# A fused attention and routed feed-forward kernel: where two late rows' slots place the score maxima of the next row

## The chip, the cores and the metric

The kernel runs on one core of one Trainium2 chip. The metric is the device time of one execution in microseconds (us); the median of three runs of the kernel before is 433.74 us.

## The reference

Eight rows (batch entries) of 256 tokens by 256 features pass through an attention layer and a feed-forward layer, each with a layer norm ahead of it and behind it:

```python
ct_q = lin(x, w_down_q); q = lin(ct_q, w_up_q) + rope(lin(ct_q, wq_r))      # 16 heads of 16
ct_kv = lin(x, w_down_kv); k = lin(ct_kv, w_up_k) + rope(lin(ct_kv, wk_r)); v = lin(ct_kv, w_up_v)
a = softmax(q @ k.T / 4) @ v ; x = x + layernorm(lin(a, wo))
logits = xn @ router_w.T                       # xn = layernorm(x); the best of 8 experts per token
shared = (silu(xn @ sg) * (xn @ su)) @ sd ; routed = expert(xn * sigmoid(top logit))
x = x + layernorm(shared + routed)
```

## The kernel before

Each of the five engines has its own instruction stream, written out in order; semaphores alone hold them together. There is no planner: the order of the work is a table per engine, and all engines walk the same tables.

**Slots and heads.** The attention part is a loop over eight slots, b = 0 to 7 (`run_attention`, L406), one for each row, and each slot has 16 heads, h = 0 to 15 (`run_slot`, L385). In head h every engine first does its `head` step: TensorE (PE) makes the scores of that head of row b in two bf16 products (L1576) and ScalarE (ACT) takes their exponentials (L873). The scores bank alternates between two, so the products of head h wait for the exponential of head h-2. Behind every fourth head PE multiplies four heads' probabilities with the values (`quad`, L1556, 16 products; here "PV").

**Maxima ahead.** The softmax subtracts a maximum that is found one slot ahead: in slot b the "units" (L367) make the scores of row b+1, 16 units a row, and in the kernel before one unit a head. A unit is two bf16 products on PE (`sm_scores`, L1517) into one of two banks and one reduction on VectorE (DVE, `sm_max`, L1057). Unit u waits for the reduction of unit u-2, which frees its bank (L1514). When eight units are reduced, GpSimd (POOL) splits that half of the maxima into three bf16 parts in four small instructions (`m_split`, L656: step M0 for the first half, M1 for the second), PE turns them (`m_turn`, L1522), ACT copies them out of the bank and issues the DMA that puts them under the queries (`mT_out`, L845). Scores of heads 0 to 7 need the first half in place, heads 8 to 15 the second.

**Other rows' steps.** Between the heads stand steps of other rows, by the tables `order` of each engine. In slot b: "A" steps make queries and keys of row b+2 (PE L1429 to L1461; ACT A_ev, A_khigh, A_qhigh, A_kmid, A_qmid; POOL A_kres, A_qres, A_klow, A_qlow; SyncE then stacks the parts in 24 DMAs, L536); "N" makes the values of row b+1; "D" finishes the attention of row b-1: D_avT0 and D_avT1 (PE turns, DVE divides, L1064 and L1068), D_aT (PE turns, ACT copies, L880), D_wo on PE (L1615, eight fp32 products, in the trace under the helper's line L1388), D_y on DVE (L1077, statistics, variance L1081), D_power on POOL (L641), D_yn on DVE (L1087), D_x1 on POOL (L675), D_stats on DVE (L991 to L1095), D_power2 on POOL; "E" takes row b-2: E_xn2 on DVE (L1104), E_xn2T on PE (in the trace under L1392), E_router. So E_xn2 of the row whose D steps are in slot b is taken in head 1 of the next slot, and PE turns it in head 3 there (in slot 7, which has its own table `last`, in head 2). An engine works its table strictly in order, within a head first the units and then the steps.

**Banks.** The turned maxima of both halves go to bank w2 (in the last row's second half to w0), which the D steps use as well; so M0 stands in head 12, behind D_wo, and PE waits there for `y_ready` (L1535).

**After the slots.** A written-out list of steps (`play`) covers the last rows' steps and the shared expert: X:n is the turn of routed token tile n on PE, x:n its copy on ACT, GR:8 gate and up products of the first routed tile, s:8 its silu, Y:n a down product.

Of the kernel before, what the change touches and what calls it, by code (L numbers as in the profile page):

```python
# [15 lines left out]

# [14 lines left out]
B, S, D = 8, 256, 256  # L31
NH, HD = 16, 16
# [84 lines left out]
def program(nc, x, const, w_down, w_q, w_kv, w_rope, w_out, w_router, bias_col, bias_v, bias_o,  # L117
# [6 lines left out]
    with ExitStack() as ctx:  # L124
# [166 lines left out]
        def m_bank(b, half):  # L291
            return w0 if (b, half) == (B - 1, 1) else w2

# [72 lines left out]

        def units(b, h):  # L367

            if b:
                return ((1, h),)
            if h < 9:
                return () if h else ((0, NH - 1),)
            u = 2 * (h - 9) + (h == NH - 1)
            return tuple((1, n) for n in range(u, u + 2 + (h >= NH - 2)))
# [6 lines left out]

        def run_slot(b, par, head, steps, order, last, behind):  # L385
            for h in range(NH):
                head(b, par, h)
                if b == B - 1:
                    play(steps, last.get(h, ""))
                    continue  # L390
                for ahead, u in units(b, h):
                    if exists(b + ahead):
                        steps["SM"](b + ahead, (par + ahead) % 2, u)
                for name in order.get(h, ()):
                    if not (b == 0 and name in MOVED):
                        step_of(steps, name, b, par)
                for n, names in FIRST_ROW.get(h, ()) if b == 0 else ():
                    for name in names.split():
                        if name in steps:
                            steps[name](n, n % 2)  # L400
                for name in MOVED:
                    if b == 0 and MOVED[name] == h and name in steps:
                        step_of(steps, name, b, par)
                behind(b, par, h)

        def run_attention(eng, head, steps, order, last, behind=lambda *_: None):  # L406

            for n, names in PROLOGUE:
                for name in names.split():
                    if name[0] == "S":
                        steps["SM"](0, 0, int(name[1:]))
                    elif name in steps:
                        steps[name](n, n % 2)
            for b in range(B):
                run_slot(b, b % 2, head, steps, order, last, behind)

# [213 lines left out]
        def _(pool):  # L633
# [38 lines left out]
            def add_x(b, par):  # L672
# [10 lines left out]
                "D_x1": add_x,  # L683
                "D_power2": lambda b, par: power("ff", b + 1, rstd2[:, ds(TB * b, TB)], var["ff"][:, :], TB),
                "SM": nothing}
            order = {0: ("M1",), 2: ("B_power",), 8: ("A_kres", "M0",),
                     9: ("A_qres",), 10: ("A_klow",), 11: ("A_qlow",), 12: ("D_power",), 13: ("D_x1",),
                     15: ("D_power2",)}

            def top_score(n, par):  # L690
# [20 lines left out]
            steps["L"] = routed_tile  # L711
            last = {0: "M1:7", 1: "E_score:0 D_power:6 D_x1:6 D_power2:6"}

            run_attention(pool, nothing, steps, order, last)
            play(steps, "D_power:7 D_x1:7 D_power2:7 E_score:1"
# [41 lines left out]
        def _(act):  # L757
# [124 lines left out]
            def xn2T_copy(b, par):  # L882
                act.wait_ge(sm["xn2T_ps"], b + 1)
                if counted(b):
# [13 lines left out]
                     5: ("A_ev0",), 6: ("A_ev1",), 7: ("A_khigh",), 8: ("A_qhigh",), 9: ("D_aT", "A_kmid",), 10: ("B_xnT", "A_qmid",),  # L898
                     12: ("C_o0",), 13: ("M0",), 14: ("B_ct",)}

            def xT_copy(seq, p):
# [18 lines left out]
            def unit_copy(seq, n, side):  # L920
# [5 lines left out]

            run_attention(act, head, steps, order, last)
            play(steps, "D_o1:7 E_xn2T:6 s:0 D_aT:7 s:1 y:0 s:2 y:1 E_xn2T:7 s:3 y:2 s:4 y:3"
                        " s:5 y:4 s:6 w:8 y:5 s:7 y:6 x:8 w:9 y:7 s:8 x:9")

# [27 lines left out]
        def _(dve):  # L958
# [149 lines left out]
            def d_router(b, par):  # L1108
# [10 lines left out]
                     6: ("D_div0",), 8: ("D_div1",), 9: ("N_v",), 11: ("D_y",),  # L1119
                     12: ("D_yn",), 14: ("D_stats",)}  # L1120


# [160 lines left out]
            steps["w"] = tile_first  # L1283
            run_attention(dve, nothing, steps, order, last)
            play(steps, "D_div0:7 c:4 c:5 E_router:6 D_div1:7 h:0 c:6 c:7 c:8 c:9 D_y:7 h:1 D_yn:7 D_stats:7 h:2 E_xn2:7"
# [97 lines left out]
        def _(pe):  # L1383
# [138 lines left out]
            def m_turn(b, par, half):  # L1522
# [8 lines left out]
                elif b < 2:  # L1531
                    if counted(2 * b):
                        pe.wait_ge(sm["mT_sb"], 2 * b)
                else:
                    pe.wait_ge(sm["y_ready"], b - 1)  # L1535
# [102 lines left out]
            def d_router(b, par):  # L1638
                pe.wait_ge(sm["xn2T_sb"], b + 1)
                for t in range(TB):  # L1640
# [11 lines left out]
                     6: ("D_avT0",), 8: ("D_avT1", "N_v",), 9: ("D_aT", "B_xnT",), 10: ("D_wo",),  # L1652
                     12: ("M0", "B_ct",), 13: ("B_ct1",)}

            def ranks(n, par):
# [151 lines left out]
            def first_routed(s, p):  # L1807
# [11 lines left out]

            run_attention(pe, head, steps, order, last, behind)  # L1820
            play(steps, "PV3:7 E_xn2T:6 D_avT0:7 E_router:6 D_avT1:7 G:1 D_aT:7 D_wo:7 U:1 Y:0 G:2 U:2 Y:1"
                        " E_xn2T:7 G:3 E_router:7 U:3 K:1 Y:2 G:4 U:4 Y:3 G:5 U:5 Y:4"
                        " G:6 U:6 I:0 Y:5 G:7 U:7 Y:6 X:8 Y:7 GR:8 X:9")

# [85 lines left out]
```

## Time and profile before

| what | before |
|---|---|
| time, median of 3 runs (lowest to highest) | 433.74 us (433.12 to 434.48) |
| time of the profiled execution | 429.76 us |
| span of the profiled execution | 427.9 us |
| TensorE busy | 397.9 us, 93% of the span |
| TensorE's granted clock, mean | 0.985 of full speed |
| VectorE, ScalarE, GpSimd busy | 273.4, 208.1, 129.6 us |

The span is from the first to the last instruction of one profiled execution; that execution's own time is 1.86 us more. Slot 5 runs in that trace from 154.2 to 178.7 us, slot 6 from there to 199.9, slot 7 up to about 219. Busy shares of TensorE are those of a pipelined engine; what it waits for is told by the idle time noted behind a group of instructions.

### The profile page before, as it was taken

How to read it: one execution, taken by the hardware profiler on the slowest of the kernel's cores; microseconds unless marked ns; L12 is line 12 of the kernel's file. 1: busy time of each engine (PE TensorE's matmuls, PEld its weight loads, DVE VectorE, ACT ScalarE, POOL GpSimd, SP SyncE). 2: the span in 40 equal slices, each digit the busy share in tenths (PEclk: the TensorE clock that was granted, in tenths of full speed). 3: DMA queues.
4: the chain of work that ended last, by engine and by line, in shares of the span. 5: the costliest groups of instructions: out<-in, count | busy, mean ns of one | idle time of the engine just before them, and what ended most of it. 6: DMA issues, size and time to landing. Idle time of an engine off the chain costs nothing.

```text
span 427.9 us, 9422 instructions
## 1 busy us (share of the span) xinstructions
PE 397.9 (93%) x3383; PEld 299.3 (70%) x3383; DVE 273.4 (64%) x629; ACT 208.1 (49%) x383; POOL 129.6 (30%) x184
## 2 busy tenths in 40 slices
PE   7998789999999999797989999999999999999990
PEld 6675456676776767374668999999994444589990
DVE  5674478787879786877475594222225898727775
ACT  1644647676675858555561112444446766311110
POOL 1423412516253434303211101212212220026872
PEclk9999899999999999899999999999999999999997
DMA  8899326364553736460127660011111111123422
GB/s 263 204 116 122 62 70 194 87 175 136 153 156 89 216 96 209 100 199 1 52 98 230 223 215 25 26 51 51 50 51 44 44 45 35 51 59 104 141 95 86
DMA packets 50756, 47.29 MB, mean 111 GB/s; under 512 B 5334, under 2 KB 45526, under 8 KB 50710
## 3 DMA queue, kind: packets, MB, share of 16 engines
q1 hardware_dynamic: 44779, 38.31, 34.2%
q0 software_dynamic: 1632, 4.46, 3.6%
q10 hardware_dynamic: 4299, 3.92, 2.7%
q8 instruction: 28, 0.46, 0.5%
q14 instruction: 18, 0.15, 0.1%
HBM read 25.19 MB, written 8.65 MB: 79 GB/s over the span
## 4 chain that ended last, share of the span: by engine, by line
PE 79%; DVE 8%; DMA 4%; issue 3%; ACT 3%; POOL 2%; ACTq 0%; DVEq 0%; POOLq 0%
PE bank L1388 40%; PE bank L1707 7%; PE bank L1392 6%; PE bank L1576 6%; PE bank L1556 5%; PE bank L1517 5%; PE bank L1732 3%; DMA stacks<-mT 2%; PE bank L1455 2%; DVE nmax L1057 2%; PE bank L1445 2%; PE bank L1503 1%; DVE wall L1087 1%; DVE stats_at L991 1%; POOL rstd_at L641 1%
## 5 line engine op out<-in xcount | busy, mean ns | idle before, releaser
L1057 DVE TENSOR_REDUCE nmax<-bank 128x2 f32<-128x512 f32 x112 | 74.4, 686 | 26.4 <-PE bank L1517 25.6
L1388 PEld LDWEIGHTS bank<-stacks,wall 128*128 128x128 f32 x512 | 59.8, 192 | 2.5 <-issue 1.9
L1388 PE MATMUL bank<-stacks,wall 128*128 128x128 f32 x512 | 61.2, 276 | 0.4 <-ACT stacks L909 0.4
L1263 DVE TENSOR_TENSOR stacks<-stacks,bank 128x512 f32<-128x512 f32 x34 | 23.3, 687 | 51.7 <-PE bank L1388 49.1
L873 ACT ACTIVATE pv<-bank 128x512 f32<-128x512 f32 x64 | 38.3, 603 | 36.7 <-PE bank L1576 35.8
L1576 PE MATMUL bank<-stacks 99*128 99x256 bf16 x256 | 49.5, 276 | 3.8 <-DMA stacks<-mT 3.3
L873 ACT ACTIVATE wall<-bank 128x512 f32<-128x512 f32 x64 | 38.5, 606 | 27.2 <-PE bank L1576 26.2
L909 ACT ACTIVATE stacks<-bank 128x512 f32<-128x512 f32 x34 | 20.3, 597 | 64.3 <-PE bank L1388 54.3
L1517 PE MATMUL bank<-stacks 96*128 96x256 bf16 x224 | 43.2, 278 | 6.4 <-DVE nmax L1057 6.2
L1388 PE MATMUL bank<-wall,stacks 128*128 128x256 f32 (+1 forms) x208 | 49.2, 380 | 0.0
L706 POOL DMA_INDIRECT stacks<-x_sc,row_i x18 | 19.9, 1105 | 89.5 <-PE bank L1392 70.5
L1388 PEld LDWEIGHTS bank<-wall,stacks 128*128 128x128 f32 x208 | 37.6, 190 | 4.1
L1576 PEld LDWEIGHTS bank<-stacks 99*128 99x128 bf16 x256 | 21.6, 100 | 26.3 <-issue 13.4
L1388 PEld LDWEIGHTS bank<-stacks,pv 128*128 128x128 f32 x320 | 37.2, 192 | 1.2 <-ACT stacks L903 0.7
L1388 PE MATMUL bank<-stacks,pv 128*128 128x128 f32 x320 | 37.4, 275 | 0.5 <-ACT stacks L903 0.5
L1707 PE MATMUL bank<-wall,stacks 128*32 x64 | 30.1, 595 | 0.5 <-ACT wdo_sb L922 0.5
L1517 PEld LDWEIGHTS bank<-stacks 96*128 96x128 bf16 x224 | 20.7, 99 | 13.7 <-DVE nmax L1057 10.8
L647 POOL TENSOR_TENSOR wall<-wall,low_sb 128x512 f32<-128x512 f32 x14 | 16.1, 1159 | 40.9 <-ACT low_sb L839 40.9
L721 POOL DMA_INDIRECT pv<-y_exp,back_i x16 | 16.2, 1010 | 33.7 <-DMA y_exp<-stacks 29.7
L1392 PE MATMUL bank<-cst,wall 128*128 128x128 f32 x160 | 24.2, 278 | 2.0 <-DVE wall L1104 0.8
L1392 PEld LDWEIGHTS bank<-cst,wall 128*128 128x128 f32 x160 | 18.0, 142 | 6.0 <-issue 2.4
L1271 DVE COPY pv<-wall 128x1024 f32 x24 | 16.7, 694 | 4.4 <-PE bank L1732 1.7
(207 smaller groups left out, 795.4 us busy)
## 6 DMA issues: line engine op xcount, KB each, us to landing
stacks<-low_sb SPq DMA_DIRECT2D x144, 64.0 KB, 2.5
wall<-gate_up SPq DMA_DIRECT2D x8, 1024.0 KB, 5.4
wall<-down SPq DMA_DIRECT2D x8, 512.0 KB, 6.9
y_exp<-stacks ACTq DMA_DIRECT2D x18, 128.0 KB, 1.7
x_tok<-wall SPq DMA_DIRECT2D x8, 256.0 KB, 2.5
stacks<-x_tok SPq DMA_DIRECT2D x16, 128.0 KB, 2.5
out<-stacks SPq DMA_DIRECT2D x8, 256.0 KB, 2.1
stacks<-low_sb SPq DMA_DIRECT2D x12, 128.0 KB, 5.9
```

What stands on the lines that cost most here:

```text
L706: pool.indirect_dma_start(out=xl[:, par, :], out_offset=None, in_=x_sc, in_offset=bass.IndirectOffsetOnAxis(ap=row_i[:, s - R0:s - R0 + 1] ...
L873: act.activation(probs[h // QUAD % 2][:, h % QUAD, :], st_bank[h % 2][:, :], ACT.Exp, scale=SCALE).then_inc(sm["exp_done"], 1)
L909: act.activation(sg, fg[:, :], ACT.Silu).then_inc(sm["sg_sb"], 1)
L1057: dve.tensor_reduce(nmax[:, half, qt, 2 * pair:2 * pair + 2], two(sm_bank[u % 2]), AX.X, ALU.max, negate=True).then_inc(sm["sm_max"], 1)
L1263: dve.tensor_tensor(to, sg, fu[:, :], ALU.mult).then_inc(sm["h_sb"], 1)
L1271: dve.tensor_copy(to, of).then_inc(sm[("gate_dve", "up_dve", "down_dve")[side]], 1)
L1388: last = pe.matmul(out_ap, lhsT, rhs, start=(n == 0), stop=(n == len(pairs) - 1))
L1392: return pe.transpose(out_ap, in_ap, ident)
L1517: last = pe.matmul(two(sm_bank[u % 2])[:, c, :], stacks[0:ROWS, par, 0, place(h), P * qt:P * qt + P], stacks[0:ROWS, par, 1, place(h), :], ...
L1556: last = pe.matmul(two(av_bank)[32 * c:32 * c + 32, g % 2, :], v_aug[:, par, k, QUAD * g + c, :], probs[g % 2][:, c, S * k:S * k + S], sta ...
L1576: last = pe.matmul(two(st_bank[h % 2])[:, k, :], stacks[0:MROWS, par, 1, place(h), P * k:P * k + P], stacks[0:MROWS, par, 0, place(h), :], ...
L1707: last = pe.matmul((fg, fu)[r][U * n:U * n + U, :], xT[:, p, P * k + U * n:P * k + U * n + U], w, start=(k == 0), stop=(k == KT - 1))
```

## The change

In slots 5 and 6 (b = B-3 and B-2) each engine uses a second table, `late`. There the units of the next row no longer come one a head but two a head in some heads, so that they end in head 10 (slot 5) and 11 (slot 6). M0 of the next row is split in head 7, turned in head 9 into bank w0 and copied in head 10. POOL splits the second half (M1) in head 12 of the same slot, ahead of D_x1, and no longer at the start of the next. The D steps and E_router move one head forward. In the last list X:9 and x:9 move ahead of GR:8 and s:8.

```diff
         def m_bank(b, half):
-            return w0 if (b, half) == (B - 1, 1) else w2
+            return w0 if (b, half) in ((B - 2, 0), (B - 1, 0), (B - 1, 1)) else w2
...
+        EVEN = at_heads(*[1] * NH)
+        UNITS_AT = {B - 3: at_heads(1, 1, 2, 1, 1, 1, 1, 2, 2, 2, 2),
+                    B - 2: at_heads(0, 1, 1, 1, 1, 2, 1, 1, 2, 2, 2, 2)}
...
             if b:
-                return ((1, h),)
+                heads = UNITS_AT.get(b, EVEN)
+                return tuple((1, u) for u in heads[h]) if h < len(heads) else ()
...
-        def run_slot(b, par, head, steps, order, last, behind):
+        def run_slot(b, par, head, steps, order, last, behind, late):
+            if b in UNITS_AT:
+                order = late
...
                 "D_power2": lambda b, par: power("ff", b + 1, rstd2[:, ds(TB * b, TB)], var["ff"][:, :], TB),
+                "M1_sixth": lambda b, par: m_split(b, par, 1) if b == B - 3 else None,
+                "N_M1": lambda b, par: m_split(b, par, 1),
...
+            late = {0: ("M1_sixth",), 7: ("M0",), 8: ("A_kres",), 9: ("A_qres",), 10: ("A_klow",), 11: ("A_qlow",),
+                    12: ("D_power", "N_M1"), 13: ("D_x1",), 15: ("D_power2",)}
...
-            last = {0: "M1:7", 1: "E_score:0 D_power:6 D_x1:6 D_power2:6"}
+            last = {1: "E_score:0 D_power:6 D_x1:6 D_power2:6"}
...
+            late = {2: ("M1",), 3: ("E_xn2T",), 4: ("D_o1",), 5: ("A_ev0",), 6: ("A_ev1",), 7: ("A_khigh",),
+                    8: ("D_aT", "A_qhigh",), 9: ("A_kmid",), 10: ("M0", "A_qmid",), 12: ("C_o0",)}
...
-                        " s:5 y:4 s:6 w:8 y:5 s:7 y:6 x:8 w:9 y:7 s:8 x:9")
+                        " s:5 y:4 s:6 w:8 y:5 s:7 y:6 x:8 w:9 y:7 x:9 s:8")
...
+            late = {1: ("A_T", "E_xn2"), 4: ("E_router",), 5: ("D_div0",), 7: ("D_div1",), 8: ("N_v",), 10: ("D_y",),
+                    11: ("D_yn",), 13: ("D_stats",)}
...
+                elif b >= B - 2:
+                    pe.wait_ge(sm["k_sb"], 2 * B)
+                    pe.wait_ge(sm["mT_sb"], 2 * b)
...
+            late = {0: ("A_R",), 1: ("A_Q",), 2: ("M1", "A_QK",), 3: ("E_xn2T",), 4: ("E_router",), 5: ("D_avT0",),
+                    7: ("D_avT1", "N_v",), 8: ("D_aT",), 9: ("M0", "D_wo",)}
...
-                        " G:6 U:6 I:0 Y:5 G:7 U:7 Y:6 X:8 Y:7 GR:8 X:9")
+                        " G:6 U:6 I:0 Y:5 G:7 U:7 Y:6 X:8 Y:7 X:9 GR:8")
```

The last five `late` tables and lists belong, in this order, to ACT (table and list), DVE (table) and PE (table and list); the one before them to POOL.

## Rows read from the trace of the kernel before

**Rows 1.** The page: busy time, share of the span, instructions of each engine.

```profile
PE 397.9 (93%) x3383; PEld 299.3 (70%) x3383; DVE 273.4 (64%) x629; ACT 208.1 (49%) x383; POOL 129.6 (30%) x184
```

**Rows 2.** PE in time: start us, us, line, what, idle before and its cause.

```profile
163.73 0.38 PE L1576 MATMUL bank<-stacks 99*128 99x256 bf16 x2
163.95 0.38 PE L1517 MATMUL bank<-stacks 96*128 96x256 bf16 x2
...
168.75 1.99 PE L1388 MATMUL bank<-wdo_sb,wall 128*128 128x256 f32 x8 [0.25 <-ACT wall L880]
...
170.80 0.38 PE L1517 MATMUL bank<-stacks 96*128 96x256 bf16 x2
...
174.55 0.39 PE L1517 MATMUL bank<-stacks 96*128 96x256 bf16 x2 [0.84 <-DVE nmax L1057]
...
176.25 0.60 PE L1517 MATMUL bank<-stacks 96*128 96x256 bf16 x2 [1.09 <-DVE nmax L1057]
176.78 1.94 PE L1556 MATMUL bank<-pv 128*32 128x256 f32 x16
...
181.83 0.66 PE L1392 MATMUL bank<-cst,wall 128*128 128x128 f32 x4 [0.23 <-DVE wall L1104]
182.41 1.07 PE L1556 MATMUL bank<-wall,pv 128*32 128x256 f32 x16
...
191.11 1.99 PE L1388 MATMUL bank<-wdo_sb,wall 128*128 128x256 f32 x8 [0.25 <-ACT wall L880]
...
196.90 0.39 PE L1517 MATMUL bank<-stacks 96*128 96x256 bf16 x2 [0.84 <-DVE nmax L1057]
...
198.60 0.39 PE L1517 MATMUL bank<-stacks 96*128 96x256 bf16 x2 [1.08 <-DVE nmax L1057]
...
202.42 0.66 PE L1392 MATMUL bank<-cst,wall 128*128 128x128 f32 x4 [0.57 <-DVE wall L1104]
```

**Rows 3.** DVE in time, slots 5 and 6.

```profile
171.22 0.69 DVE L1057 TENSOR_REDUCE nmax<-bank 128x2 f32<-128x512 f32 x1 [1.68 <-PE bank L1517]
171.83 0.68 DVE L1077 TENSOR_TENSOR wall<-bank,bo_sb 128x512 f32<-128x512 f32 x1
...
173.81 0.68 DVE L1057 TENSOR_REDUCE nmax<-bank 128x2 f32<-128x512 f32 x1
...
175.51 1.28 DVE L1057 TENSOR_REDUCE nmax<-bank 128x2 f32<-128x512 f32 x2
...
194.19 0.68 DVE L1077 TENSOR_TENSOR wall<-bank,bo_sb 128x512 f32<-128x512 f32 x1
...
196.08 0.17 DVE L1081 TENSOR_SCALAR var_at<-mv_at 128x2 f32<-128x2 f32 x1
```

**Rows 4.** Windows: us, busy us of PE, PEld, DVE, ACT, POOL, granted clock, DMA.

```profile
172.00:176.00 4.00, 2.32 (x20) 1.23 (x16) 3.57 (x10) 2.59 (x6) 1.03 (x2) 1.00 0.41 103
176.00:180.00 4.00, 3.75 (x27) 1.68 (x28) 2.85 (x9) 0.98 (x3) 2.31 (x6) 0.57 0.36 89
...
194.00:198.00 4.00, 2.68 (x28) 1.29 (x20) 3.57 (x11) 2.24 (x5) 0.70 (x1) 1.00 0.00 0
198.00:202.00 4.00, 3.26 (x40) 1.37 (x40) 3.41 (x10) 1.85 (x5) 2.44 (x4) 1.00 0.01 3
```

**Rows 5.** ACT in time, end of slot 5.

```profile
174.39 0.73 ACTq L859 DMA_DIRECT2D stacks<-mT  x1
175.22 1.08 ACT L873 ACTIVATE wall<-bank 128x512 f32<-128x512 f32 x2 [0.86 <-PE bank L1576]
```

**Rows 6.** POOL in time: first and last instruction of one split of maxima.

```profile
179.06 0.20 POOL L663 CAST mparts<-nmax 128x16 bf16<-128x16 f32 x1
...
179.90 0.22 POOL L669 TENSOR_TENSOR mparts<-nres,mparts 128x16 bf16<-128x16 f32 x1
```

**Rows 7.** PE in time at the first routed tiles.

```profile
273.43 0.82 PE L1388 MATMUL bank<-stacks,pv 128*128 128x128 f32 x5 [0.47 <-ACT stacks L903]
```

More of the change, by code:

```diff
@@ L15 @@
 from contextlib import ExitStack
+from itertools import accumulate
 import numpy as np
@@ L365, in step_of, with at_heads @@
                 steps[name](b + ahead, (par + ahead) % 2)
+        def at_heads(*counts):
+            ends = list(accumulate(counts))
+            assert ends[-1] == NH
+            return [range(e - c, e) for c, e in zip(counts, ends)]
+        EVEN = at_heads(*[1] * NH)
+        UNITS_AT = {B - 3: at_heads(1, 1, 2, 1, 1, 1, 1, 2, 2, 2, 2),
+                    B - 2: at_heads(0, 1, 1, 1, 1, 2, 1, 1, 2, 2, 2, 2)}
         def units(b, h):
             if b:
-                return ((1, h),)
+                heads = UNITS_AT.get(b, EVEN)
+                return tuple((1, u) for u in heads[h]) if h < len(heads) else ()
             if h < 9:
@@ L404, in run_slot, with run_attention @@
                 behind(b, par, h)
-        def run_attention(eng, head, steps, order, last, behind=lambda *_: None):
+        def run_attention(eng, head, steps, order, last, behind=lambda *_: None, late=None):
             for n, names in PROLOGUE:
@@ L417, in run_attention @@
             for b in range(B):
-                run_slot(b, b % 2, head, steps, order, last, behind)
+                run_slot(b, b % 2, head, steps, order, last, behind, late or order)
         def nothing(*_):
@@ L711, in _ @@
             steps["L"] = routed_tile
-            last = {0: "M1:7", 1: "E_score:0 D_power:6 D_x1:6 D_power2:6"}
-            run_attention(pool, nothing, steps, order, last)
+            last = {1: "E_score:0 D_power:6 D_x1:6 D_power2:6"}
+            run_attention(pool, nothing, steps, order, last, late=late)
             play(steps, "D_power:7 D_x1:7 D_power2:7 E_score:1"
@@ L925, in _ @@
             last = {2: "D_o1:6", 3: "E_xn2T:5", 5: "M1:7", 6: "D_aT:6", 10: "C_o0:7"}
-            run_attention(act, head, steps, order, last)
+            run_attention(act, head, steps, order, last, late=late)
             play(steps, "D_o1:7 E_xn2T:6 s:0 D_aT:7 s:1 y:0 s:2 y:1 E_xn2T:7 s:3 y:2 s:4 y:3"
-                        " s:5 y:4 s:6 w:8 y:5 s:7 y:6 x:8 w:9 y:7 s:8 x:9")
+                        " s:5 y:4 s:6 w:8 y:5 s:7 y:6 x:8 w:9 y:7 x:9 s:8")
             def body(seq, n, p, kinds):
@@ L1283, in _ @@
             steps["w"] = tile_first
-            run_attention(dve, nothing, steps, order, last)
+            run_attention(dve, nothing, steps, order, last, late=late)
             play(steps, "D_div0:7 c:4 c:5 E_router:6 D_div1:7 h:0 c:6 c:7 c:8 c:9 D_y:7 h:1 D_yn:7 D_stats:7 h:2 E_xn2:7"
@@ L1818, in _ @@
                     7: "D_wo:6", 8: "K:0", 9: "PV1:7 Ga:0", 10: "Gb:0", 11: "Ua:0", 12: "Ub:0", 13: "PV2:7"}
-            run_attention(pe, head, steps, order, last, behind)
+            run_attention(pe, head, steps, order, last, behind, late=late)
             play(steps, "PV3:7 E_xn2T:6 D_avT0:7 E_router:6 D_avT1:7 G:1 D_aT:7 D_wo:7 U:1 Y:0 G:2 U:2 Y:1"
                         " E_xn2T:7 G:3 E_router:7 U:3 K:1 Y:2 G:4 U:4 Y:3 G:5 U:5 Y:4"
-                        " G:6 U:6 I:0 Y:5 G:7 U:7 Y:6 X:8 Y:7 GR:8 X:9")
+                        " G:6 U:6 I:0 Y:5 G:7 U:7 Y:6 X:8 Y:7 X:9 GR:8")
             def body(seq, n, p, kinds):
```

## The prediction

> **What bounds the kernel now.** I read the page first: TensorE is busy 93% of the span [rows 1], so the time is its work plus the places where it is held. Nothing in the change takes work from it: the same units, turns and products are issued. Its effect is therefore the sum of the holds that go and the holds that come. For these I read PE in time over slots 5 and 6, looking only at groups with idle time before them [rows 2]. In each slot's end two units wait for a reduction: 0.84 and 1.09 us in slot 5, 0.84 and 1.08 us in slot 6. The next hold is in the following slot, where the turn E_xn2T waits for DVE's normalised row: 0.23 us before 181.83 and 0.57 us before 202.42. DVE in time [rows 3] says why the units wait. The reduction at 173.81 could have run at 172.8, but D_y and its statistics (from 171.83) stand ahead of it; the next pair (175.51) stands behind D_yn. So two chains share DVE at a slot's end: unit to reduction to unit, which holds PE, and D_wo, D_y, D_power, D_yn, D_x1, D_stats, D_power2, E_xn2, E_xn2T, which holds PE one slot on. The reader should see that the second one is the one that ends last: its whole length from D_y to the turn is 202.42 - 194.19 = 8.23 us in slot 6, of which D_y to the variance at 196.08 is 1.9 us. Between variance and turn only one slot edge lies, and PE arrives before the turn is ready in both slots.
>
> **Part 1: units two a head.** This removes the four holds in the slot ends, 0.84 + 1.09 + 0.84 + 1.08 = 3.85 us. That is the cover that goes from in front of E_xn2T, and what is late next is E_xn2T itself. To see how late, I walk slot 5 forward with these intervals: scores or a unit on PE take 0.22 us start to start (163.73 to 163.95 in [rows 2]); a unit's reduction can start 0.42 us after the unit (170.80 to 171.22 in [rows 2, 3]); reductions follow each other in 1.28 - 0.68 = 0.61 us and the unit that waits for one starts 0.06 us behind its end (173.81 + 0.68 = 174.49, unit 174.55); a PV group is 1.00 us, D_wo 1.83 to the next product, and D_y can start 2.03 us after D_wo begins.
>
> Two units a head are no longer spaced by PE's other work, so the second must wait for the reduction of unit u-2. In slot 5, head 7, unit 9 waits for the reduction of unit 7, which stands on DVE behind D_div0: about 0.75 us of hold on PE. PE then does unit 9, D_avT1, N_v, PV, head 8, units 10 and 11, D_aT, head 9, units 12 and 13, M0, and only then D_wo. Compared with before, D_wo has one head's scores less, but three units (0.66) and M0's turn (0.21 to 0.3) more ahead of it; with the hold it begins at 170.3 where it began at 168.75 [rows 2], 1.5 us later. D_y may start at 172.3. But it stands on DVE behind the reductions of units 14 and 15, whose products come behind D_wo and head 10: 172.35 + 0.42, two intervals, and D_y begins at 173.95 where it began at 171.83 [rows 3]. From there the chain is free of reductions: 8.23 us by slot 6 of before, and it ends at 182.2, against 181.83. So slot 5 gives up 0.4 us at the point where PE is held, although PE gets through heads 11 to 15 sooner and would be at that turn at 180.6.
>
> Slot 6 by the same walk: everything starts 0.4 later at its E_xn2T. Holds on paired units: D_avT1 waits for D_div0, which stands behind two reductions, 0.4; unit 7 0.15; unit 11 0.4. With M0's turn (0.3) D_wo begins at 192.6, before 191.11 [rows 2]. D_y could start at 194.6, but units 12 and 13 come from PE only behind D_wo (194.6 and 194.85), their reductions stand ahead of D_y and the first waits 0.42: D_y begins at 196.25, before 194.19. The reductions of 14 and 15 stand between the variance (198.15) and D_yn, and delay it by 0.3; POOL's split, below, adds 0.2. The turn of row 5 in slot 7 is ready at 196.25 + 8.23 + 0.5 = 205.0, against 202.42. That is **+2.6 us**, and it holds the 0.4 of slot 5. PE would be there at 202.8 and waits 2.2 us. Slot 7 is written as before and each of its later steps hangs on this turn or stands behind it on PE, so I let the 2.6 us pass whole to the end. The bounds: 0 if slot 7 takes it all up, 3.9 us if slot 5's 0.4 is doubled by slot 6's and each of the four removed holds comes back as a reduction wait.
>
> **Part 2: M0 in head 9, in bank w0.** No instruction is added; the turn moves from head 12 to 9, ahead of D_wo, and its 0.3 us stands in the sum above. Its DMA issue on ACT takes 0.73 us and moves ahead of A_qmid and the exponential of head 11 [rows 5]; with D_aT ahead of A_qhigh, row 7's parts for the queries reach POOL about 2 us later. POOL's A_qlow then ends at 176.0, just as D_power wants the engine, and the stack of DMAs for row 7 ends near 179.3, where unit 0 is wanted at 178.7: a wait of 0.6, hidden in front of the late E_xn2T. The scores of heads 0 wait for a DMA that now has three heads more: that costs nothing, and gave nothing before.
>
> **Part 3: M1 split a slot sooner.** Four POOL instructions from 179.06 to 179.90 + 0.22, 1.06 us [rows 6], now stand between D_power and D_x1. D_yn leaves POOL about 1.0 us of idle time there, so the cost is 0 to 0.1 in slot 5. In slot 6 the split waits for the reduction of unit 15 (199.5): D_x1 is 0.2 late, counted above. At the slot's start nothing on PE waited for the split, so its gain is 0. If D_yn came with no delay of its own, the split would cost up to 1.1.
>
> **Part 4: D steps and router a head sooner.** They issue the same instructions; what matters is in part 1: a head sooner in name is later in time, because the heads are fuller.
>
> **Part 5: X:9 ahead of GR:8.** Before, PE waited 0.47 us for the copy x:9 [rows 7]. Now the turn stands ahead of sixteen gate products and more, and the copy is hidden by them; the token tile had been in memory for some us. Gain 0.47, bounds 0 and 0.5.
>
> **The clock.** At the slot ends PE is sparse: 2.32 us busy in 172 to 176, then the granted clock in 176 to 180 is 0.57, nearly the lower level of 1.2 GHz, and a PV group takes 1.94 instead of 1.07 us [rows 4, 2]. After 2.68 busy us in 194 to 198 it stayed at 1.00, the level of 2.4 GHz [rows 4]. So one of two such stretches cost clock: 0.43 of 4 us, 1.7 us. In my walk the stretches ahead of both turns are emptier than either (about 1.9 of 3.7 us, then 1.3 of 3.6), and come where nothing else hides slow products. The bounds are 0 (one dip, as now) and 3.4 less the 1.7 of before plus 0.9 of cover lost, 2.6. I take half of one dip, **+0.85**: one more dip falls on the path and half of it lies in front of waits.
> The Trainium skill, in "TensorE: Matmul & The Clock Gate" (Part 1: The HAM clock gate), says that idling is what lowers the clock and that sustained activity must come first for it to rise. The two windows agree with the first only half, since one of two sparse stretches kept its clock. By the rule alone both turns would be followed by slow products, which is the third rival below.
>
> **Sum.** +2.6 - 0.45 + 0.85 = +3.0 us. Made against the profiled execution (429.76 us, 427.9 of it span) it gives 432.8; that execution is 4.0 us under the median of the runs, of which the profile shows no cause, and I carry the difference over: 433.74 + 3.0 = 436.7.
>
> **Rivals.**
> *The chain is not late.* If DVE takes the paired reductions without holding PE, D_wo keeps its place, and D_y's turn comes before the reductions that I put ahead of it, then PE's arrival decides: slot 6's turn comes at 180.6 instead of 181.83 and slot 7's at 201.2 instead of 202.42, 1.2 us sooner, and with X:9 -1.7: 432.0. It decides from the point where E_xn2 is done before PE arrives: my walk misses that by 1.6 us in slot 6 and by 2.2 in slot 7. For it: the holds of 3.85 us are real, and they do go. Against it: D_y has waited for its reduction even at one unit a head [rows 3].
> *Slot 7 or the reductions take up most of it.* Half of 2.6 us arrives, X:9 gives its part and no dip is added: +0.85, 434.6, no difference to be told. For it: 0.57 of PE's wait in slot 7 was there before; my intervals add up over forty steps.
> *Both turns are followed by low clock.* +2.6 - 0.45 + 2.6 = +4.75: 438.5. For it: the emptier stretches. Against it: slots 6 to 7 in the trace.
> *The change does nothing in the slots* (only X:9 counts): 433.3; it would need the 0.4 and 2.6 us both to be errors.
>
> **Chances.** About 0.3% (1.3 us) is what a measurement of this kernel can tell from none. My forecast (435.2 to 437.8) 0.43; both dips 0.18; slot 7 takes it up 0.14; nothing in the slots 0.07; not late 0.18. Slower then 0.61, the same 0.21, faster 0.18. The range leaves a tenth at each end: from 432.2, nearly the case where the chain is not late, to 439.2, both dips with a margin of 0.7. The likeliest sign's own range is 435.2 to 439.2.
>
> **What the next profile would show.** Right: no hold on units in the slot ends; holds of a few tenths on the second unit of heads 7 to 10; D_wo at about 170.3 and 192.6; D_y behind two reductions; PE idle over 1 us before E_xn2T near 182.2 and over 2 us near 205.0, and a granted clock under 0.8 behind one of them; no wait for the copy of X:9. Wrong: E_xn2T starting right behind the unit ahead of it; D_wo earlier than 169.5; D_y starting as soon as D_wo is done; slot 7 beginning and ending closer together than the 2.6 us allow.

## The result, and the profile after

The changed kernel takes 436.28 us (median of 14 runs, 433.26 to 441.68); the kernel before took 431.84 us in the 14 runs beside it (430.98 to 434.48). The ratio is 1.0096, 95% interval [1.0071, 1.0121]: slower, by 3.1 to 5.2 us. Executions more than 1.5% above the fastest of their kernel (two of these 14) are left out of the ratios and of the means further down. The profiled executions have spans of 434.9 us (mean granted clock 0.979) and 427.9 us (0.985).

First the page after, to be read beside [rows 1]:

```profile
PE 401.8 (92%) x3383; PEld 299.9 (69%) x3383; DVE 274.7 (63%) x629; ACT 208.1 (48%) x383; POOL 129.8 (30%) x184
```

The same 3383 products are issued; busy time grew 3.9 us without one product more (the mean clock is lower in this execution), and the span grew 7.0. The rest is waiting. Where, PE in time says (slots 5 and 6 of the changed kernel; columns as in [rows 2]):

```profile
155.61 0.39 PE L1598 MATMUL bank<-stacks 99*128 99x256 bf16 x2
...
166.54 0.39 PE L1536 MATMUL bank<-stacks 96*128 96x256 bf16 x2 [0.60 <-DVE nmax L1074]
...
171.70 1.99 PE L1407 MATMUL bank<-wdo_sb,wall 128*128 128x256 f32 x8
...
176.78 0.88 PE L1598 MATMUL bank<-stacks 99*128 99x256 bf16 x4 [0.88 <-ACT pv L888]
178.24 0.39 PE L1598 MATMUL bank<-stacks 99*128 99x256 bf16 x2 [0.58 <-ACT wall L888]
...
181.83 0.39 PE L1536 MATMUL bank<-stacks 96*128 96x256 bf16 x2 [1.65 <-DMA stacks<-low_sb]
...
183.91 0.96 PE L1411 MATMUL bank<-cst,wall 128*128 128x128 f32 x4 [0.49 <-DVE wall L1121]
184.80 1.93 PE L1578 MATMUL bank<-wall,pv 128*32 128x256 f32 x16
...
195.92 1.99 PE L1407 MATMUL bank<-wdo_sb,wall 128*128 128x256 f32 x8
...
199.14 0.39 PE L1536 MATMUL bank<-stacks 96*128 96x256 bf16 x2 [0.35 <-DVE nmax L1074]
...
202.15 0.39 PE L1598 MATMUL bank<-stacks 99*128 99x256 bf16 x2 [0.47 <-ACT wall L888]
203.12 0.39 PE L1598 MATMUL bank<-stacks 99*128 99x256 bf16 x2 [0.58 <-ACT wall L888]
...
208.64 0.65 PE L1411 MATMUL bank<-cst,wall 128*128 128x128 f32 x4 [2.26 <-DVE wall L1121]
...
277.80 4.96 PE L1407 MATMUL bank<-stacks,pv 128*128 128x128 f32 x43
```

The holds of 0.84 to 1.09 us in front of units [rows 2] are gone from both slot ends. In their place PE now waits further on: for the exponentials of the scores (0.88, 0.58, 0.47, 0.58), for the transfer of the low parts (1.65), and above all in front of the turn E_xn2T of row 5 (2.26, before 0.57). The 0.47 us of [rows 7] do not appear behind the early X:9.

Slot 5 begins at 155.61, before at 154.21. These 1.40 us arose where nothing was changed: a low clock (0.53) from 33.8 to 41 put this execution 2.76 us behind, and one in the kernel before, at 44 to 52 (0.80 and 0.77 in its two halves), gave half of that back. I subtract the 1.40 to compare. D_wo then stands at 170.30 and 194.52 (before 168.75 and 191.11). DVE in time, same kernel:

```profile
174.17 1.29 DVE L1074 TENSOR_REDUCE nmax<-bank 128x2 f32<-128x512 f32 x2 [1.27 <-PE bank L1536]
175.38 0.68 DVE L1094 TENSOR_TENSOR wall<-bank,bo_sb 128x512 f32<-128x512 f32 x1
...
198.39 1.29 DVE L1074 TENSOR_REDUCE nmax<-bank 128x2 f32<-128x512 f32 x2 [1.27 <-PE bank L1536]
199.60 0.68 DVE L1094 TENSOR_TENSOR wall<-bank,bo_sb 128x512 f32<-128x512 f32 x1
...
201.57 1.28 DVE L1074 TENSOR_REDUCE nmax<-bank 128x2 f32<-128x512 f32 x2
202.77 0.87 DVE L1104 SCALAR_TENSOR_TENSOR wall<-wall,mv_at,rstd_at 128x256 f32<-128x256 f32 x2
```

D_y is at 173.98 and 198.20 (before 171.83 and 194.19 [rows 3]), each time straight behind a pair of reductions. POOL in time shows what else stands in that chain: the split of the second maxima ends just as D_yn is done, and D_x1 follows it:

```profile
202.92 0.38 POOL L674 CAST mparts<-nmax 128x16 bf16<-128x16 f32 x1 [0.48 <-DVE nmax L1074]
...
204.06 0.22 POOL L680 TENSOR_TENSOR mparts<-nres,mparts 128x16 bf16<-128x16 f32 x1
204.24 1.27 POOL L686 TENSOR_TENSOR x_sb<-x_sb,wall 128x512 f32<-128x512 f32 x1
```

D_yn ends at 202.77 + 0.87 = 203.64, so D_x1 is 0.6 us late. Last the windows of the changed kernel (columns as in [rows 4]): from slot 5's start to E_xn2T of row 4, from there to E_xn2T of row 5, and four stretches of 4 us.

```profile
155.61:183.91 28.30, 23.80 (x208) 15.47 (x205) 19.91 (x47) 17.59 (x36) 10.59 (x20) 1.00 0.47 132
183.91:208.64 24.73, 20.43 (x174) 11.77 (x174) 15.83 (x36) 11.96 (x22) 4.60 (x11) 0.93 0.30 95
176.00:180.00 4.00, 2.54 (x26) 1.07 (x26) 2.16 (x8) 3.27 (x8) 3.35 (x7) 1.00 0.39 99
180.00:184.00 4.00, 1.86 (x15) 0.95 (x14) 2.89 (x9) 1.93 (x4) 1.47 (x2) 1.00 0.33 81
184.00:188.00 4.00, 4.00 (x30) 2.21 (x30) 1.33 (x3) 1.89 (x4) 0.00 (x0) 0.57 0.40 100
204.00:208.00 4.00, 2.39 (x34) 0.87 (x26) 1.46 (x6) 2.32 (x5) 2.16 (x3) 1.00 0.00 0
208.00:212.00 4.00, 2.98 (x28) 2.20 (x32) 1.77 (x6) 1.89 (x4) 0.00 (x0) 1.00 0.12 46
```

The same two stretches of the kernel before, and of the kernel that only has the early X:9 (its code in these slots is that of before):

```profile
154.21:181.83 27.62, 25.11 (x211) 16.31 (x207) 20.39 (x48) 17.47 (x36) 10.25 (x20) 0.94 0.51 143
181.83:202.42 20.59, 17.86 (x172) 11.42 (x172) 15.36 (x35) 11.24 (x22) 4.33 (x10) 1.00 0.32 104
```

```profile
156.85:183.65 26.80, 23.85 (x211) 15.95 (x207) 20.36 (x48) 17.46 (x36) 10.22 (x20) 1.00 0.51 142
183.65:205.03 21.38, 19.21 (x173) 11.81 (x173) 15.30 (x35) 10.71 (x20) 4.54 (x11) 0.92 0.35 107
```

From slot 5's start to E_xn2T of row 5: 53.03 us changed, 48.21 before, 48.18 in the third, each with one stretch of low clock. That is +4.8 us over before; PE's idle time in them is 48.21 - 42.97 = 5.2 us before and 53.03 - 44.23 = 8.8 changed. Behind the first routed tiles the distance has shrunk by 0.7 (from 6.23 us there to 5.49). In the last output tiles this one execution loses another 1.5, in waits that no step of the change touches; I did not find their cause.

### The profile page after: what moved, and what is told of

Its sections match the earlier page's. It is cut to its first block, busy times and chain, and to the rows that moved or that the text cites. A ratio compares the mean times of both kernels' runs of the same rounds, so it can differ in the third digit from the quotient of the medians.

```text
span 434.9 us, 9422 instructions
## 1 busy us (share of the span) xinstructions
PE 401.8 (92%) x3383; PEld 299.9 (69%) x3383; DVE 274.7 (63%) x629; ACT 208.1 (48%) x383; POOL 129.8 (30%) x184
## 4 chain that ended last, share of the span: by engine, by line
PE 70%; DVE 11%; POOL 5%; issue 5%; DMA 4%; ACT 3%; SPq 1%; ACTq 1%; DVEq 0%; POOLq 0%
PE bank L1407 36%; PE bank L1731 7%; PE bank L1411 5%; PE bank L1578 4%; PE bank L1598 4%; PE bank L1536 4%; PE bank L1756 3%; DVE nmax L1074 3%; PE bank L1474 2%; PE bank L1522 1%; PE bank L1464 1%; SPq L547 1%; DMA stacks<-mT 1%; DVE stacks L1377 1%; POOL pv L736 1%
## 5 line engine op out<-in xcount | busy, mean ns | idle before, releaser
L1536 PE MATMUL bank<-stacks 96*128 96x256 bf16 x224 | 41.7, 274 | 5.9 <-DVE nmax L1074 4.0
L1536 PEld LDWEIGHTS bank<-stacks 96*128 96x128 bf16 x224 | 19.8, 98 | 14.6 <-DVE nmax L1074 9.6
```

The source lines that it names most:

```text
L1536: last = pe.matmul(two(sm_bank[u % 2])[:, c, :], stacks[0:ROWS, par, 0, place(h), P * qt:P * qt + P], stacks[0:ROWS, par, 1, place(h), :], ...
```

## The experiments

The last two columns of this table come from the list of each kernel's executions, which gives the span S and the mean granted clock c (as a share of full speed) of each. S(1-c) is the **lost clock**, Sc the span without it; means over the runs, with their standard error. The experiments ran in three sets of four, each with its own runs of the kernel before beside it, whose Sc and lost clock were 421.1 ± 0.2 and 9.9 ± 0.5 (x9_only to dy_first), 421.7 ± 0.2 and 9.2 ± 0.3 (pack_only to mild), 421.5 ± 0.1 and 9.5 ± 0.3 (the last four). So a difference between kernels of different sets is uncertain by another 0.5 us or so. The split is rough: across the runs of one kernel 1 us of lost clock goes with 0.5 to 1.0 us of span. The traces show one reason, that a low clock in front of a wait costs less: the 1.7 us lost in slot 5 of before (0.43 of 4 us) made the way to the turn of row 4 only 0.8 us longer (27.62 for the 26.80 of the third kernel).

```
kernel        median us   ratio to before [95%]       Sc            lost clock
changed       436.28      1.0096 [1.0071, 1.0121]     424.8 ± 0.2    9.2 ± 0.5
x9_only       432.31      0.9986 [0.9956, 1.0015]     420.5 ± 0.3   10.3 ± 0.5
even_units    434.16      1.0026 [0.9992, 1.0061]     422.0 ± 0.4   10.0 ± 0.6
m1_late       438.35      1.0142 [1.0085, 1.0199]     423.7 ± 0.5   13.0 ± 1.2
dy_first      438.24      1.0146 [1.0084, 1.0207]     424.4 ± 0.5   11.5 ± 1.6
pack_only     433.76      1.0020 [0.9985, 1.0054]     422.0 ± 0.3    9.8 ± 0.6
steps_only    433.52      1.0000 [0.9969, 1.0032]     421.7 ± 0.3    9.5 ± 0.4
slot6_even    434.52      1.0043 [1.0013, 1.0072]     422.9 ± 0.4    9.5 ± 0.6
mild          431.75      0.9959 [0.9924, 0.9995]     421.0 ± 0.3    8.2 ± 0.7
turn_later    435.17      1.0047 [1.0015, 1.0078]     423.5 ± 0.3   10.2 ± 0.6
act_order     435.96      1.0082 [1.0047, 1.0116]     424.3 ± 0.4    9.5 ± 0.6
filled        430.55      0.9950 [0.9922, 0.9979]     421.4 ± 0.2    7.5 ± 0.4
combined      432.37      0.9985 [0.9955, 1.0016]     420.7 ± 0.2    9.4 ± 0.4
```

**x9_only.** The kernel before with X:9 ahead of GR:8, and the copy ahead of s:8 on ACT.

```diff
-" G:6 U:6 I:0 Y:5 G:7 U:7 Y:6 X:8 Y:7 GR:8 X:9"
+" G:6 U:6 I:0 Y:5 G:7 U:7 Y:6 X:8 Y:7 X:9 GR:8"
```

> The kernel before with X:9 ahead of GR:8 and x:9 ahead of s:8, nothing else. If the slots alone make the change slower, this one is 0.5 to 0.75 us faster than before (the wait of 0.47 us on PE goes, and the first routed tiles begin 0.7 us sooner behind the inverse). If the swap brings a new hold (the copy standing ahead of the silu), it is equal or slower.

0.9986 [0.9956, 1.0015]. The size agrees with the 0.47 us of [rows 7], the interval also with nothing. Sc is 0.7 ± 0.4 us lower. So the loss is in the slots. Against this kernel it is 4.0 us by the medians and 4.7 by the ratios.

**even_units.** The changed kernel with one unit a head in both slots; the second split back at its old place.

```diff
-UNITS_AT = {B - 3: at_heads(1, 1, 2, 1, ...), B - 2: at_heads(0, 1, 1, ...)}
+UNITS_AT = {B - 3: EVEN, B - 2: EVEN}
-late = {0: ("M1_sixth",), 7: ("M0",), ... 12: ("D_power", "N_M1"), ...}
+late = {0: ("M1",), 7: ("M0",), ... 12: ("D_power",), ...}
```

> The changed kernel with one unit a head as before and M1 split at the next slot's start as before; bank w0, M0 in head 9, the D steps a head sooner and X:9 stay. Theory (packed units hold PE and stand ahead of D_y): it falls to 0.5 to 1.5 us under before, D_y of slot 5 begins about 0.4 us sooner than in the kernel before, the units' holds of about 1 us come back in the slot ends. Rival (the moved steps, the DMA issue on ACT ahead of A_qmid, or bank w0 cost the time): it stays 2 to 4 us above before.

434.16 us; 1.0026, 2.1 us of median under the changed kernel and 1.9 over x9_only. Its trace has the holds of units back (0.97 and 0.91, 0.79 and 1.08 us). So the kernel that has those waits again is the faster one, and the packed spacing costs. The time lies between the two expectations, under the rival's and over the theory's: what stands beside the packing seems to cost something too, but against x9_only the intervals overlap.

**m1_late.** The changed kernel, units still packed, the second split back in the next slot's head 0.

> The changed kernel with M1 split at the next slot's start as before, all else changed. Theory (D_y behind the reductions is most of it, the split adds its wait ahead of D_x1): 0.3 to 0.6 us under the changed kernel, E_xn2T of row 5 still over 1.5 us late. Rival (the split is what delays the chain): 2 us or more under the changed kernel.

438.35 us, 2.1 over the changed kernel by the medians, where 0.3 to 0.6 under it was expected; the intervals of the ratios overlap. PE in time:

```profile
180.64 0.39 PE L1536 MATMUL bank<-stacks 96*128 96x256 bf16 x2 [1.73 <-DMA stacks<-low_sb]
182.69 0.39 PE L1559 MATMUL bank<-idb,mparts 128*24 128x128 bf16 x2 [1.21 <-POOL mparts L680]
...
209.83 0.66 PE L1411 MATMUL bank<-cst,wall 128*128 128x128 f32 x4 [1.75 <-DVE wall L1121]
```

The turn of the second maxima now waits 1.21 us for the split, while E_xn2T of row 5 waits 0.5 us less than in the changed kernel (1.75 for 2.26). The two columns part here: without lost clock this kernel is 1.1 ± 0.5 us shorter than the changed one, with 3.9 ± 1.3 us more of lost clock. So the early split saves a wait of 1.21 us, and a later one is longer with it (the low clock of this trace, from 180 to 194, may have a part in that). Whether it is worth anything is not shown: the higher median goes with the lost clock of six runs, and no run says whether the new wait brought it.

**dy_first.** m1_late with D_y and D_yn a head earlier on DVE, ahead of the reductions that they stood behind.

```diff
-8: ("N_v",), 10: ("D_y",), 11: ("D_yn",)
+8: ("N_v",), 9: ("D_y",), 10: ("D_yn",)
```

> The kernel of m1_late with D_y on DVE in head 9 and D_yn in head 10, so that the reductions of units 14 and 15 (slot 5) and 12 to 15 (slot 6) stand behind D_y; units stay two a head. Theory (the place of D_y behind the reductions costs about 1.6 us a slot): D_y of slot 5 begins 2.03 us after D_wo, and the time is 1.5 to 3 us under m1_late. Rival (the holds on PE from paired units, or the late stack of DMAs, cost the time): within 0.7 us of m1_late.

PE in time, slot 6 and the turn of row 5:

```profile
199.97 0.39 PE L1536 MATMUL bank<-stacks 96*128 96x256 bf16 x2 [1.88 <-DVE nmax L1074]
...
207.05 0.60 PE L1411 MATMUL bank<-cst,wall 128*128 128x128 f32 x4
```

The wait at E_xn2T is gone, and a unit waits 1.88 us instead; from slot 5's start to this turn it is 52.59 us, changed 53.03. At 438.24 us it is no faster than m1_late, where the theory wanted 1.5 to 3 us. The two chains on DVE trade places: with the reductions first the turn waits (1.75 in m1_late), with D_y first a unit does (1.88).

**pack_only** and **steps_only.** x9_only with the packed units and nothing else; and x9_only with D_avT, N_v, D_aT, D_wo, D_y and the router a head sooner and units as before.

> The kernel of x9_only (the one before with X:9 moved) with the units of slots 5 and 6 two a head as in the change, all step tables, banks and splits as before. Theory (packed units hold PE in pairs and put reductions ahead of D_y): 1.5 to 3 us over x9_only, of the 3.8 that the whole change costs beyond X:9. Rival (the packing is harmless by itself and the other moves cost the time): within 0.7 us of x9_only.

> The kernel of even_units with M0 back in heads 8, 12 and 13 and in bank w2, so that beside X:9 only the D steps, N_v and the router stand a head sooner. even_units was 1.5 us over x9_only. Theory (M0 ahead of D_wo and its DMA issue ahead of A_qmid on ACT make that): 0 to 0.7 us over x9_only. Rival (the steps a head sooner make it, by the wait of N_v for ACT's copy and of D_avT1 for D_div0): still 1 to 2 us over x9_only.

433.76 and 433.52 us: 1.4 and 1.2 over x9_only by medians (1.5 and 0.6 by ratios, intervals overlapping). The waits of pack_only:

```profile
177.48 0.61 PE L1577 MATMUL bank<-stacks 99*128 99x256 bf16 x4 [1.44 <-DMA stacks<-mT]
...
180.00 0.39 PE L1538 MATMUL bank<-idb,mparts 128*24 128x128 bf16 x2 [0.83 <-POOL mparts L670]
...
201.74 0.61 PE L1577 MATMUL bank<-stacks 99*128 99x256 bf16 x4 [1.03 <-DMA stacks<-mT]
...
205.44 0.66 PE L1393 MATMUL bank<-cst,wall 128*128 128x128 f32 x4 [1.76 <-DVE wall L1105]
```

Without the early M0 the scores of the next slot wait for the transfer of the maxima (1.44, 1.03): the changed kernel has no such wait. Neither part alone costs what the whole does, and pack_only stands at the lower edge of what was expected; even_units less steps_only, the early M0 and its bank, is 0.6 by medians. The three add up to 3.2 of the 4.0 us, but each of them is about as large as the uncertainty of a median, so this list is a rough one.

**slot6_even.** The changed kernel, slot 6 alone with one unit a head; row 7's second split is back at the start of slot 7.

> The changed kernel with one unit a head in slot 6 (its M1 split at the start of slot 7); slot 5 as changed. By the prediction's walk slot 6 makes 2.2 of the 2.6 us: then 1.5 to 2.5 us under the changed kernel. Rival: the cost is split evenly between the slots, and about 1 us comes off.

434.52 us, 1.8 under the changed kernel (intervals [1.0013, 1.0072] and [1.0071, 1.0121] barely touch; Sc is 1.9 ± 0.5 lower). Its E_xn2T of row 5 waits 0.24 us and not 2.26. So the spacing in slot 6, with the early split of row 7 that goes with it, makes nearly half of the loss.

**turn_later.** The changed kernel with row 5's turn E_xn2T behind D_avT1 of row 6 in the last slot; D_avT0, which now comes first, gets a wait of its own for D_y of the row before.

```diff
-last = {1: "PV3:6", 2: "E_xn2T:5", 3: "D_avT0:6", 4: "M1:7 D_avT1:6", ...}
+last = {1: "PV3:6", 3: "D_avT0:6", 4: "M1:7 D_avT1:6 E_xn2T:5", ...}
```

> The changed kernel with one step moved on TensorE: the turn of row 5's normed tile (E_xn2T, in slot 7) stands behind the second D_avT of row 6 at head 4, and not at head 2; its copy on ScalarE goes from head 3 to head 5. In the changed kernel TensorE waits 2.26 us for VectorE at this turn (208.64). Theory: this wait is the price of the late D chain of row 5, and work that is ready could stand in it; then the wait falls under 0.3 us and the kernel comes out 1.5 to 2.2 us under the changed one, at about 434.3. Rival: the wait hides later ones in the last slot (unit holds, the routed part's start), or the clock decides; then within 0.5 us of the changed kernel.

```profile
211.20 0.66 PE L1411 MATMUL bank<-cst,wall 128*128 128x128 f32 x4 [0.96 <-ACT wall L881]
...
212.91 1.09 PE L1411 MATMUL bank<-cst,wall 128*128 128x128 f32 x8 [0.63 <-DVE wall L1085]
```

435.17 us, 1.1 under the changed kernel, less than expected. The wait for VectorE's E_xn2 is gone, but the turn of the attention row that now comes first waits 0.96 us for ACT's copy, and the pair behind it 0.63. Further on the router's products wait 0.61 us for ACT (216.64), where in the changed kernel D_wo waited 0.36. Up to the first gate products the changed kernel waited 2.26 + 0.38 + 0.36 = 3.00 us, this one 2.20, and the way there from the PV group ahead of the first of these waits is 0.81 us shorter (12.79 from 208.63, 13.60 from 204.99), and Sc fell by 1.3 ± 0.4 (the intervals of the ratios still overlap by a hair). So the late chain of row 5 does cost time at the end, and this move fills only a part of the wait that it gives PE.

**act_order.** The changed kernel, high and middle parts of q ahead of the copies of D_aT and M0 on ACT.

```diff
-8: ("D_aT", "A_qhigh",), 9: ("A_kmid",), 10: ("M0", "A_qmid",)
+8: ("A_qhigh", "D_aT",), 9: ("A_kmid",), 10: ("A_qmid", "M0",)
```

> The changed kernel with two pairs exchanged on ScalarE in slots 5 and 6: the high parts of q (A_qhigh) ahead of the copy of D_aT in head 8, and the middle parts (A_qmid) ahead of the copy of M0 in head 10. It lets the low parts and their transfers start earlier by a copy or two. In the changed kernel unit 0 of row 7 waits 1.65 us for the transfer of the stacked low parts (181.83), and E_xn2T of row 4 behind it still 0.49 us for VectorE. Theory: the transfer's wait stands in front of a D chain that is as late, so it costs nothing; then within 0.5 us of the changed kernel, and the wait moves to E_xn2T. Rival: the transfer's wait is a cost of its own; then 1 to 1.5 us under the changed kernel.

```profile
182.78 0.66 PE L1411 MATMUL bank<-cst,wall 128*128 128x128 f32 x4 [0.61 <-DVE wall L1121]
```

```profile
154.53:182.78 28.25, 25.21 (x209) 15.97 (x205) 19.77 (x47) 17.60 (x36) 10.62 (x20) 0.94 0.45 133
182.78:205.93 23.15, 18.85 (x174) 11.20 (x175) 15.84 (x36) 11.94 (x22) 4.59 (x11) 1.00 0.32 101
```

The wait of 1.65 us for the low parts is gone, E_xn2T of row 4 comes 28.25 us behind slot 5's start (154.53), changed 28.30, and the median is 0.3 us lower. The longest single wait that the change brought to slot 5 was free: it stood in front of a later one. In this trace the low clock also falls ahead of the turn of row 4, and slot 6 has none: its 23.15 us to the turn of row 5 are the changed kernel's slot 6 at full clock.

**mild.** x9_only with two units in head 10 only, and none in head 15, in both slots.

> The kernel of x9_only with one unit moved: in slots 5 and 6 head 10 has two units, ahead of D_wo, and head 15 none; all else as before. DVE is idle 1.7 us behind D_wo there, so the eleventh reduction costs nothing, and the wait of the last unit for D_yn's row goes. Theory (what decides is which reductions stand ahead of D_y, and where DVE is idle): 0.5 to 2 us under x9_only. Rival (any unit ahead of D_wo delays the chain as much as it frees): equal or slower than x9_only.

```profile
175.02 0.39 PE L1518 MATMUL bank<-stacks 96*128 96x256 bf16 x2 [0.83 <-DVE nmax L1058]
...
177.54 0.39 PE L1577 MATMUL bank<-stacks 99*128 99x256 bf16 x2 [0.90 <-DMA stacks<-mT]
178.63 0.47 PE L1518 MATMUL bank<-stacks 96*128 96x256 bf16 x2 [0.70 <-DMA stacks<-low_sb]
```

431.75 us, 0.9959 [0.9924, 0.9995]: one hold of 0.83 instead of two in each slot, D_y not delayed, and transfers that now show (in slot 6 the turn of row 5 waits 1.56 us). Faster than the kernel before; not told apart from x9_only.

**combined.** mild with the first maxima turned in head 10, and turn_later's move.

> Mild spacing of the units (one a head up to head 9, two in head 10, none in head 15), X:9, the first maxima turned in head 10 behind D_wo into the bank w0 with its copy in head 11, and row 5's E_xn2T in slot 7 moved from head 2 to head 4 as in turn_later; all D steps stay at their old heads. Theory: what holds the mild kernel still is the wait of 1.56 us at E_xn2T of row 5 and the waits of 0.90 and 0.70 us for transfers that follow the maxima; with both eased it comes out 0.5 to 1.5 us under mild, at 430.3 to 431.3. Rival: the last slot's waits or the transfers take it up; then within 0.4 us of mild.

432.37 us, 0.6 over mild by the medians, where 0.5 to 1.5 under it was expected. The rival was nearer: unit 0 of the next row waits 1.73 us for the low parts, and no gain over mild is left.

**filled.** x9_only, with products that nobody reads in the idle time in front of units 14 and 15.

```diff
+if b >= B - 2 and u >= NH - 2:
+    pe.wait_ge(sm["v_ready"], b + 1)
+    for _ in range(10 if u == NH - 2 else 14):
+        pe.matmul(w1[:, 0:P], ones_bf[:, :], ones_bf[:, :], start=True, stop=True)
 pe.wait_ge(sm["sm_max"], ...)
```

> The kernel before with the early unit of slot 7 (X:9), and besides with 10 products of 128 x 128 ahead of unit 14 and 14 ahead of unit 15 in slots 5 and 6, into a bank that nothing reads: they fill most of the idle time in which TensorE waits for a score unit's maxima at a slot's end. Theory (the sparse stretch at the slot's end brings the low clock about 176 to 180 on some executions): the low clock there goes, the mean of the lost clock falls by 0.5 to 1.5 us, and the kernel comes out as much under x9_only, at 431 to 432. Rival: the lost clock is set by something else in the program; then no change against x9_only, or up to 1 us slower where the products delay the units.

PE in time at the end of slot 5, then two windows:

```profile
174.16 0.72 PE L1517 MATMUL bank<-ones_bf 128*128 128x128 bf16 x10
175.16 0.39 PE L1521 MATMUL bank<-stacks 96*128 96x256 bf16 x2 [0.28 <-DVE nmax L1057]
175.38 0.38 PE L1580 MATMUL bank<-stacks 99*128 99x256 bf16 x2
175.61 0.94 PE L1517 MATMUL bank<-ones_bf 128*128 128x128 bf16 x14
176.85 0.39 PE L1521 MATMUL bank<-stacks 96*128 96x256 bf16 x2 [0.30 <-DVE nmax L1057]
```

```profile
172.00:176.00 4.00, 3.72 (x50) 2.58 (x43) 3.57 (x10) 2.19 (x6) 0.90 (x2) 1.00 0.41 103
176.00:180.00 4.00, 3.20 (x38) 1.64 (x35) 3.64 (x10) 2.02 (x4) 2.18 (x4) 1.00 0.33 82
```

430.55 us, 0.9950 [0.9922, 0.9979]: the lowest median of all, faster than both kernels, 1.8 us under x9_only (their intervals overlap a little, as do those of filled and mild). It brings no unit forward: unit 14 stands 20.33 us behind the start of slot 5 (154.83), before 20.34. Against x9_only, what fell is the lost clock, from 10.3 ± 0.5 to 7.5 ± 0.4 us, a difference of 2.8 ± 0.6, while Sc rose by 1.0 ± 0.4. Those two ran in different sets; against the kernel before beside it the lost clock fell by 2.0 ± 0.5 and Sc stayed (421.4 and 421.5). The traces agree on the place: of the 14 kernels' profiled executions, only that of filled has its full clock all through slots 5 and 6; each of the other 13 has a stretch of low clock between 176 and 212 us. So the holds at the slot ends did cost something beside the waiting itself: they are sparse stretches, and slow products follow, as far as one trace of each kernel and the means of the lost clock can show it.

## Why the prediction was right, point by point

The forecast was 436.7 us, slower; measured 436.28. The mechanism was right: the chain to E_xn2T came late, by the reductions ahead of D_y, and PE waited there. That the figure came within 0.4 us is luck. Two terms were off in size and in part set each other off, and the base was high: I added +3.0 to a median of 433.74, which more runs put at 431.8 to 433.0, while the added time is 3.1 to 5.2.

**Part 1, the late D chain: right, under-sized.** Slot 5 came out as walked: D_wo 170.30 (walked 170.3), D_y 173.98 (173.95), E_xn2T 182.51 (182.2), the hold on the second unit 0.60 (0.75). In slot 6, D_wo came at 194.52 where I had 192.6: the low clock behind 184 lies in it (192.6, 0.3 for slot 5 and some 1.7 for 0.43 of 4 us make 194.6). PE's wait at the turn of row 5 is 2.26 (2.2). The wait at the turn of row 4 was forecast at over 1 us and is 0.49, because 1.65 us went to the transfer ahead of it. turn_later and slot6_even show that the wait of row 5 reaches the end, dy_first that putting D_y first on DVE does not win it back. The term of +2.6 was too small. The failed step is the comparison: I took "E_xn2T at 181.83" as what slot 5 of before takes, but that slot held a dip of the clock (176 to 180 at 0.57 [rows 4]). The same code without a dip takes 26.80 us to that turn (x9_only), not 27.62. Against 28.30 the loss of slot 5 alone is +1.5, not +0.4. The rows of before already held the hint: from D_y to the turn slot 5 took 181.83 - 171.83 = 10.00 us, slot 6 only the 8.23 that I carried over. For slot 6 at full clock there are two traces: 23.15 us in act_order, and in filled, whose steps of the slots are those of before, 20.56 (181.61 to 202.17). That is +2.6, where I had 2.2. Together the slots cost 1.5 + 2.6 = 4.1 us in the traces and 4.3 ± 0.4 by the means of Sc (changed less x9_only), for the 2.6 of the forecast.

**Part 2, the early M0: right for itself, blind to its gain.** The wait for the low parts came, 1.65 us for the 0.6 forecast, and is hidden as said (act_order). But "gave nothing before" is true only of the kernel before: with packed units and M0 at its old place PE waits 1.44 and 1.03 us for the maxima's transfer (pack_only).

**Part 3, the early split: its gain of 0 stays open.** With packed units 1.21 us of wait return without it (m1_late), and 0.5 us of a later one go; by the medians that kernel is 2.1 us slower, without lost clock it is 1.1 shorter. Its cost was under-sized: D_x1 is late by 0.6 in slot 6, 0.2 forecast.

**Part 4.** Costed at nothing beside part 1; steps_only puts it at 0.6 us (ratios) to 1.2 (medians) over x9_only with the old units, which is not told apart from none.

**Part 5, X:9: right.** The wait of 0.47 is gone, the distance between the traces shrinks by 0.7 there; the time of x9_only agrees, but is not told apart from no gain.

**The clock: +0.85 was wrong.** One stretch of low clock lies behind the turn of row 4 (0.57 in 184 to 188), none behind that of row 5, after 2.39 busy us of 4. That is one dip, as before, and the mean lost clock is 9.2 ± 0.5 (10.1 ± 0.8 over all 14 runs) against 9.5 ± 0.3: no change that can be told. I had priced the change in sparse stretches from two windows of one execution.
The Trainium skill, in "TensorE: Matmul & The Clock Gate" (Part 1: The HAM clock gate), says that idling is what lowers the clock; filled agrees with it (less idling, 2.0 to 2.8 us less lost clock). Which stretch is followed by the low clock can't be told from its busy time here: after 2.39 busy us of 4 (204 to 208, changed kernel) the clock stayed at 1.00, after 2.32 (172 to 176, before) it fell to 0.57.

**The rivals.** "Not late" and "nothing in the slots" fall with the 2.26 us and the 4.7 us over x9_only. "Slot 7 takes it up" falls with the distance of the traces: 6.22 us at the turn of row 5 and 6.23 just ahead of the routed tiles. "Both turns followed by low clock" didn't come in the profiled execution.

## What to carry to other kernels

Before a hold is removed, ask what the engine runs into next, and what the work that is brought forward takes from an engine that two chains share: here 3.85 us of holds went, PE's idle time over two slots still rose from 5.2 to 8.8 us, and neither order tried on DVE gave both chains their turn. When a walk is compared with a trace, first look whether the stretch it is compared with had its full clock; a dip in it hides as much of a loss as the dip cost. And a wait that can't be removed may still be worth filling with products that nobody reads, if the engine's clock falls behind it.

## What I had not expected

The largest gain found, 0.5%, is in executing more: with 48 products that nobody reads the lost clock is 2.0 ± 0.5 us (against before) to 2.8 ± 0.6 us (against x9_only) lower and the time about 2 us. Low clock is not a fixed property of the code: with the same instructions in the slots the dip was at 176 to 180 in the execution of before, and in slot 6 in that of x9_only (0.92 over 183.65 to 205.03). Where it falls matters as well: act_order and the changed kernel each lost about 1.7 us of clock in slots 5 and 6, act_order in front of the turn of row 4, where a wait hid it (28.25 + 23.15 = 51.40 us to the turn of row 5), the changed kernel behind it (53.03). The two kernels differ only in two exchanges on ACT, so about the same loss of clock cost 1.6 us in one place and next to nothing in the other.
